# A graph network with routed experts on one core: four PSUM banks for the next table's chunks, one-hots handed over by rising counts, the second layer's weights summed on VectorE

## The reference

```python
xn = _layernorm(x, axis=-1)
# graph part, for l in range(2), on xn:
W = jnp.einsum('rb,bio->rio', coeffs[l], bases[l])      # 8 relations from 30 bases
h = jnp.einsum('ni,rio->rno', x, W)
msg = h[edge_type, src] * deg_inv[dst][:, None]
agg = jax.ops.segment_sum(msg, dst, num_segments=num_nodes)
x_new = agg + x @ self_loops[l]                         # relu after the first layer
# attention part, on xn: q, k = elu(.) + 1; kv = k^T v; out = q kv / (q . k_sum)
x = x + graph(xn) + attention(xn)
# experts, on layernorm(x): idx = argmax(xf @ router_w.T + router_b)
x = x + relu(relu(xf @ W1[idx] + b1[idx]) @ W2[idx] + b2[idx])
```

## Time and profile before

| | |
|---|---|
| median of 3 runs | 3629.47 us (3622.14 to 3641.18) |
| the profiled execution | 3602.8 us, its span 3601.1 us |
| granted TensorE clock, mean | 0.822 |
| busy | PE 68%, PEld 49%, DVE 26%, ACT 18%, POOL 46% |
| startup | 0 to 385 us |
| first layer | 385 to 1985 us |
| second layer | 1985 to 3275 us |
| experts | 3340 to 3601 us |

### The profile page before, as it was taken

One profiled execution on the slowest core, in us unless ns is written; L12 is line 12 of the kernel. 1 busy time (PEld: TensorE's weight loads), 2 busy tenths in 40 slices (PEclk: granted clock), 3 DMA queues, 4 the chain that ended last, 5 costly groups with the idle time before them and its releaser, 6 DMA issues. The chain is left out here.

```text
span 3601.1 us, 37652 instructions
## 1 busy us (share of the span) xinstructions
PE 2442.1 (68%) x9592; PEld 1750.2 (49%) x9592; DVE 924.5 (26%) x2885; ACT 657.0 (18%) x1423; POOL 1648.2 (46%) x1712
## 2 busy tenths in 40 slices
PE   6999356667666667766669166666766666657197
PEld 3777234445444445444446154544545445445065
DVE  2120112222222222222223032332323323224233
ACT  4455111111111111111112001111112111110033
POOL 0000554455444554444540655555655556652534
PEclk9999778888888888888889577777777878778577
DMA  8655533333333333333331323333332333321441
GB/s 221 223 222 190 163 105 110 111 105 115 109 106 105 105 117 107 111 110 106 114 111 73 110 84 89 88 90 87 89 92 85 91 91 89 92 82 45 130 128 53
DMA packets 155518, 401.32 MB, mean 111 GB/s; under 512 B 35102, under 2 KB 86657, under 8 KB 140348
## 3 DMA queue, kind: packets, MB, share of 16 engines
q0 software_dynamic: 81648, 219.65, 21.0%
q10 hardware_dynamic: 36156, 126.22, 9.1%
q1 hardware_dynamic: 37585, 53.92, 5.5%
HBM read 262.69 MB, written 141.04 MB: 112 GB/s over the span
## 5 line engine op out<-in xcount | busy, mean ns | idle before, releaser
L487 POOL DMA_INDIRECT gnn_ring<-table,g_idx x1564 | 1511.8, 967 | 1604.7 <-PE gnn_pagg L530 840.0
L530 PE MATMUL gnn_pagg<-gnn_ring,gnn_oh 128*128 x3904 | 1125.3, 432 | 387.4 <-issue 337.2
L530 PEld LDWEIGHTS gnn_pagg<-gnn_ring,gnn_oh 128*128 128x128 f32 x3904 | 779.5, 213 | 723.0 <-issue 615.3
L514 DVE TENSOR_TENSOR gnn_oh<-gnn_col,g_dst 128x256 f32<-128x256 f32 x976 | 408.0, 425 | 1510.9 <-DVEq L49 1344.8
L711 PE MATMUL gnn_pm<-gnn_whigh,gnn_high 128*128 128x512 f32 x392 | 209.0, 533 | 369.2 <-ACT gnn_rows L762 269.1
L711 PEld LDWEIGHTS gnn_pm<-gnn_whigh,gnn_high 128*128 128x128 f32 x392 | 98.7, 252 | 422.1 <-ACT gnn_rows L762 291.0
L1014 ACT ACTIVATE gnn_qe<-gnn_pq,gnn_bq 128x128 f32<-128x128 f32 x98 | 36.0, 367 | 1062.9 <-remote 1019.0
L711 PE MATMUL gnn_pm<-gnn_wlow,gnn_high 128*128 128x512 f32 x392 | 195.2, 498 | 0.0
L711 PE MATMUL gnn_pm<-gnn_whigh,gnn_low 128*128 128x512 f32 x392 | 194.7, 497 | 0.0
L762 ACT COPY gnn_rows<-gnn_pm 128x512 f32<-128x512 f32 x196 | 110.7, 587 | 449.4 <-DMA pre_bs<-in_L_gnn_bases 257.1
L366 PE MATMUL pre_psum<-pre_whigh,pre_high 128*128 128x512 f32 x392 | 159.4, 407 | 10.6 <-DVE pre_low L294 7.0
(11 more groups left out here) (172 smaller groups left out, 2320.0 us busy)
## 6 DMA issues: line engine op xcount, KB each, us to landing
table<-pre_rows ACTq DMA_DIRECT2D x49, 1024.0 KB, 3.9
table<-gnn_rows ACTq DMA_DIRECT2D x48, 1024.0 KB
gnn_ring<-table,g_idx POOLq DMA_INDIRECT x1564
pre_bs<-in_L_gnn_bases SPq DMA_DIRECT2D x64, 240.0 KB
bucket<-gnn_zrow SPq DMA_DIRECT2D x16, 650.0 KB
g_xT<-bucket SPq DMA_DIRECT2D x20, 520.0 KB, 6.3
x1T<-gnn_x1T ACTq DMA_DIRECT2D x49, 128.0 KB
gnn_x1T<-x1T ACTq DMA_DIRECT2D x49, 128.0 KB
```

Of the source, the lines that this page charges most:

```text
L487: eng.indirect_dma_start(self.ring[:, q % RG, t, 0:D], None, self.g.table[self.l][:, :], bass.IndirectOffsetOnAxis(ap=self.g.idx[:, at:at ...
L514: self.nc.vector.tensor_tensor(self.oh[:, h, :, :], self.col[:, :].unsqueeze(1).to_broadcast([P, n, P]), self.g.dst[:, ds(q * TPG + h * n, ...
L530: mm = nc.tensor.matmul(pagg[:, k, 0:self.width], self.oh[:, h, i, :], self.ring[:, ds(q & (RG - 1), 1), t, 0:self.width].rearrange("p o n ...
```

## The change

1. The products of a block in the first layer get four PSUM banks, one for each chunk (`pm`, `NC = 4`). `chunk_free` and its waits are gone. The transposes `pT` lose their own bank and are written to the fourth bank of `pm`; `turn(b)` waits for `rows_ok` of the block before. `pagg` has one bank in place of two in the first layer.
2. `oh_ok` and `oh_free` are no more decremented: their counts rise through the layer, and the loops wait for `q + b + 1`, worked out from the loop's register. `pairs` is gone; the gate waits for `oh_free` of the second half.
3. The second layer's relation weights (used in `gnn_first`) are made on VectorE: 240 terms, base times coefficient added to a tile `wr` that stays in SBUF, spread over the startup's blocks: 7 beside most blocks, 3 or 1 beside those with layernorm work, 0 beside two. `wrel`'s second half, its 8 pieces on TensorE and ScalarE and its reload are gone. SyncE loads 30 whole bases.
4. In `gnn_first` VectorE makes the weights' low part behind block 0, and TensorE waits for it ahead of block 1.

The core of the diff:

```diff
     def onehots(self, eng, b, seq):
             for h in range(HALF):
-                take(eng, self.oh_free[h])
+                eng.wait_ge(self.oh_free[h], q + b + 1)
...
     (sum)
             for h in range(HALF):
-                take(eng, self.oh_ok[h])
+                eng.wait_ge(self.oh_ok[h], q + b + 1)
                 for i in range(n):
...
-                    if t == 0:
-                        mm.then_inc(self.pairs, 1)
-                    elif i == n - 1:
-                        mm.then_inc(self.oh_free[h], 1)
+                mm.then_inc(self.oh_free[h], 1)
...
     (gathers)
-                eng.wait_ge(self.pairs, last)
+                eng.wait_ge(self.oh_free[HALF - 1], last)
...
     (gnn_first)
-        pm = s.ps("pm", [P, W, 512])
+        pm = s.ps("pm", [P, NC, 512])
-        pT = s.ps("pT", [P, 512])
+        pT = pm[:, NC - 1, 0:D]
...
-            def multiply(k):
+            def multiply(b):
                 reach(eng, low_ok)
-                for n in range(2 * W):
-                    reach(eng, chunk_free)
+                for n in range(NC):
...
-            def turn():
+            def turn(b):
                 reach(eng, xn_ok)
+                if b:
+                    eng.wait_ge(rows_ok, b)
...
-            eng.wait_ge(wr_in, WEIGHTS_IN)
             for h in range(H2):
-                nc.scalar.copy(whigh[:, h, :], rows[:, h, :]).then_inc(split_ok, 1)
+                nc.scalar.copy(whigh[:, h, :], wr[:, h, :]).then_inc(split_ok, 1)
...
     (startup)
+        def terms_beside(b):
+            return 0 if b in (0, 2 * G) else 1 if chunk_at(b) else 3 if chunk_at(b - 1) else 7
...
+            def terms(lo, hi):
+                for i in range(lo, hi):
+                    n, r = divmod(i, R)
+                    if r == 0:
+                        eng.wait_ge(base_in[n % AT_ONCE], 16 * (n // AT_ONCE + 1))
+                        if n:
+                            eng.wait_ge(added, n)
+                        else:
+                            eng.wait_ge(cr_in, 16)
+                    w = wr[:, :, r * D:(r + 1) * D]
+                    if n:
+                        ins = V.scalar_tensor_tensor(out=w, in0=base[:, n % AT_ONCE, :, :], scalar=cr[:, i:i + 1], in1=w,
+                                                     op0=ALU.mult, op1=ALU.add)
+                    else:
+                        ins = V.tensor_scalar(w, base[:, 0, :, :], cr[:, i:i + 1], None, ALU.mult)
+                    if r == R - 1:
+                        ins.then_inc(added, 1)
...
                 multiply(b)
-                if piece_after(b) is not None:
-                    weights(piece_after(b))
                 if b + AHEAD < NB:
                     turn(b + AHEAD)
```

More of the change, by code:

```diff
@@ L96, in __init__ @@
         self.dve_own, self.scattered = s.sem("dve_own"), s.sem("scattered")
-        self.agg_sems = {n: s.sem(n) for n in ("groups_in", "gate", "ring_ok", "agg_ok", "agg_free",
-                                               *(f"oh_ok{h}" for h in range(HALF)), *(f"oh_free{h}" for h in range(HALF)))}
+        self.agg_sems = {n: s.sem(n) for n in ("groups_in", "gate", "ring_ok", "agg_ok", "agg_free")}
         dram = lambda name, shape, dt: nc.dram_tensor(name, shape, dt).ap()
@@ L184, in startup @@
         dve_own = g.dve_own
-        bases = [a["L0_gnn_bases"][l].rearrange("b (q i) o -> q b (i o)", q=4) for l in range(2)]
+        cr_in, added = s.sem("cr_in"), s.sem("added")
+        base_in = [s.sem(f"base_in{k}") for k in range(AT_ONCE)]
+        bases = a["L0_gnn_bases"][0].rearrange("b (q i) o -> q b (i o)", q=4)
         block = ctx.enter_context(nc.Block())
@@ L197, in stage @@
             return xs[0:4 * R, at:at + PIECE // D, :].rearrange("p b d -> p (b d)")
-        def piece_after(b):
-            c, late = divmod(b - EVERY - 1, EVERY)
-            return NPC + c if late == 0 and 0 <= c < NPC else None
+        def terms_beside(b):
+            return 0 if b in (0, 2 * G) else 1 if chunk_at(b) else 3 if chunk_at(b - 1) else 7
+        first_terms = [min(NBASE * R, sum(terms_beside(c) for c in range(b))) for b in range(NB + 1)]
+        assert first_terms[NB] == NBASE * R
+        done_beside = [next(b for b in range(NB) if first_terms[b + 1] >= R * (n + 1)) for n in range(NBASE)]
+        base_at = [max(n, done_beside[n - AT_ONCE] + 1) if n >= AT_ONCE else n for n in range(NBASE)]
         @block.sync
@@ L235, in _ @@
                     rows_in(b // G + 2)
-                if b % EVERY == 2 and b // EVERY < NPC:
-                    load(NPC + b // EVERY)
+                if b == 0:
+                    eng.dma_start(cr[:, :], a["coeff_rows"].rearrange("(o n) -> o n", o=1).to_broadcast([P, NBASE * R])).then_inc(cr_in, 16)
+                for n in range(NBASE):
+                    if base_at[n] == b:
+                        if n >= AT_ONCE:
+                            eng.wait_ge(added, n - AT_ONCE + 1)
+                        eng.dma_start(base[:, n % AT_ONCE, :, :], a["L0_gnn_bases"][1][n].rearrange("(h p) o -> p h o", p=P)
+                                      ).then_inc(base_in[n % AT_ONCE], 16)
         @block.gpsimd
@@ L332, in _ @@
                     edges()
+                terms(first_terms[b], first_terms[b + 1])
+            eng.wait_ge(added, NBASE)
         @block.tensor
@@ L396, in weights @@
             def weights(n):
[L397 to L400 removed]
+                if n >= WB:
+                    eng.wait_ge(w_out[n % WB], 16 * (n // WB))
                 for q in range(4):
@@ L443, in _ @@
                 eng.wait_ge(stored[k], 16 * ((NB + 1 - k) // 2))
-            for k in range(WB):
-                eng.wait_ge(w_out[k], 16 * (NPC // WB + (NPC // 2 if k < 2 else 0)))
 class Aggregate:
@@ L462, in __init__ @@
         self.agg_ok, self.agg_free = sems["agg_ok"], sems["agg_free"]
-        self.oh_ok = [sems[f"oh_ok{h}"] for h in range(HALF)]
-        self.oh_free = [sems[f"oh_free{h}"] for h in range(HALF)]
+        self.oh_ok = [s.sem(f"oh_ok{h}") for h in range(HALF)]
+        self.oh_free = [s.sem(f"oh_free{h}") for h in range(HALF)]
     def groups_of(self, eng, b):
@@ L499, in begin @@
             ins.then_inc(self.ring_ok, 1)
-    def end(self, eng):
-        for h in range(HALF):
-            take(eng, self.oh_free[h])
     def onehots(self, eng, b, seq):
@@ L663, in _ @@
             seq(ins)
-            for h in range(H2):
-                eng.wait_ge(split_ok, h + 1)
-                ins = V.tensor_tensor(wlow[:, h, :], rows[:, h, :], whigh[:, h, :], ALU.subtract)
-            ins.then_inc(split_ok, 1)
             eng.wait_ge(kv_in, 80)
@@ L670, in _ @@
                 step(b, b % 2)
-            agg.end(eng)
+                if b == 0:
+                    for h in range(H2):
+                        eng.wait_ge(split_ok, h + 1)
+                        ins = V.tensor_tensor(wlow[:, h, :], wr[:, h, :], whigh[:, h, :], ALU.subtract)
+                    ins.then_inc(split_ok, 1)
             eng.wait_ge(kv_done, 1)
@@ L1268, in program @@
         had = nc.snapshot_sems()
-        startup(nc, g, a)
-        nc.clear_and_free_semaphores(nc.allocated_since(had))
-        nc.all_engine_barrier()
-        gnn_first(nc, g, a)
+        with nc.sbuf_tensor("second_wr", [P, H2, R * D], F32) as wr:
+            startup(nc, g, a, wr)
+            nc.clear_and_free_semaphores(nc.allocated_since(had))
+            nc.all_engine_barrier()
+            gnn_first(nc, g, a, wr)
         r = Routed(Scope(nc, ctx, "rt"))
```

108 lines of the change are left out of this document (48 added, 60 removed).

## The result

| | before | changed |
|---|---|---|
| median | 3625.8 us (3619.0 to 3641.18, 4 runs) | 3484.89 us (3471.86 to 3495.94, 4 runs) |
| profiled execution, span | 3602.8, 3601.1 us | 3479.84, 3477.8 us |

What follows compares the result with a forecast made beforehand. TensorE bounds the startup; in the first layer nothing does, as TensorE's messages come late in gather bursts. Startup -30, first layer's start 0, four banks -181, gate -25: -236, so 3629.5 becomes 3393 us; range 3240 to 3520.

Steps and rivals of the forecast that it cites:

- Startup, -30: Startup: eight weight pieces leave TensorE's path, VectorE's terms at 0.689 us each stay hidden: -30 us (to +80).
- Start of the first layer, 0 (-10 to +7): First layer's block 0: TensorE starts some 10 us sooner, but the chain ends by the burst's end anyway: 0.
- Four banks: First layer: the product's 24 matmuls run unbroken, period falls from 31.8 to 27.5 us over 42 periods: -181 us.
- a: First layer: lateness of L537's message after the loop, 3.1 us before, taken as 6 on average; 3 best.
- from there to the product: First layer: the way from VectorE's first use (L633) to the product (L711), taken as 4.3 us.
- a clock above 0.92: First layer, profile after: TensorE's clock was to rise above 0.92, from 0.86, as a sign of success.
- Quick and slow blocks mix: First layer: a longer block gets its gate in quiet time and is early again; period between 24.4 and 31.8 us.
- Counts, 0: Both layers' 490 groups: the gap of 0.54 us may grow or shrink by 0.1, +-49 us; taken as 0.
- Gate in the second layer, -25: Second layer: gathers' gate opens 0.8 us sooner at each of 49 gates, between -39 and 0: -25 us.
- rival 1: First layer: the wait moves to L537's message, a is 10, period 31.5 us; 3580 us, chance 0.18.
- Rival 2: First layer: L537's message waits for the burst's full release, period 36.6 us; slower, 3776 us, chance 0.10.
- Rival 3: Startup: VectorE becomes the bound, a term costing over 0.75 us; at 1.0 us +59, 3480 us, chance 0.06.

Runs made afterwards that it cites:

- b: The changed kernel with the four banks undone, counts and VectorE's weights kept, on a chip with prompt messages: 2587.8 us, ratio 0.9917 to the kernel before.
- c: The changed kernel with four banks and counts both undone, only VectorE's weights kept, on a chip with prompt messages: 2582.0 us, ratio 0.9895 to the kernel before.
- g: The changed kernel as it is, run again on a chip with late messages: 3353.3 us, ratio 0.9323 to the kernel before.
- i: The changed kernel with the first layer's transposes put ahead of the projection, on a chip with late messages: 3373.9 us, ratio 0.9396 to the kernel before.
- s: The changed kernel with the four banks undone, counts and VectorE's weights kept, on a chip with late messages: 3471.3 us, ratio 0.9643 to the kernel before.
- t: The changed kernel in which the projection sends no message of its own, on a chip with late messages: 3381.6 us, ratio 0.9395 to the kernel before.
- h: The changed kernel with the one-hot counts undone, four banks and VectorE's weights kept, on a chip with late messages: 3417.1 us, ratio 0.9489 to the kernel before.

## Why the prediction was right or wrong

**Startup, -30: right.** It gave 27.0 us. The term of a weight was put too low, 0.689 where it took 0.748 us, so a plain block has 7 x 0.748 + 0.42 = 5.66 us of VectorE work in a TensorE block of 5.65. The cover is gone to the last tenth; TensorE still was busy 243 of 250 us. An eighth term would have made VectorE the bound.

**Start of the first layer, 0 (-10 to +7): wrong, +9.** TensorE did start sooner, and with it block 0's loop went into the first burst from its 8th microsecond. Four rows of the changed kernel:

```profile
365.62 0.21 PE L542 MATMUL gnn_pagg<-g_zero 128*128 128x2 bf16 x1
399.44 0.42 DVE L533 TENSOR_TENSOR gnn_oh<-gnn_col,g_dst 128x256 f32<-128x256 f32 x1 [10.78 <-DMA g_bound<-bounds]
412.37 0.21 PE L553 MATMUL gnn_pagg<-g_zero 128*128 128x2 bf16 x1
434.36 0.16 DVE L647 TENSOR_SCALAR gnn_dm<-gnn_pagg 128x1 f32<-128x1 f32 x1 [24.00 <-remote]
```

The loop took 46.8 us where it had taken 12.4, and L647 then came 22 us late where it had been 14. VectorE's 4.49 us for the low parts now stood in the chain ahead of block 1 as well. The step said that the chain ends by the burst's end whatever its start. Here ScalarE had the transposes 93.5 us after the first gather, at the end of the burst, and the product and the low parts came behind it; before it had them 67.2 us after. No run separates the early start from the low parts.

**Four banks: the mechanism right, its neighbour missed.** The wait between the chunks went, and I asked what is late next. I named L537's message and nothing else, and put the way from there to the product at a fixed 4.3 us. In the block shown it is 9.1 us, because the transposes' message is late as well, and the product itself takes 8.1 where I had 6.2, much of it at the low clock. The working, in us:

| term | forecast | block shown | mean of 44 periods | the same before |
|---|---|---|---|---|
| loop | 10.9 | 9.6 | 11.5 | 10.6 |
| a, to VectorE's first use | 6 | 3.3 | 4.2 | 2.4 |
| from there to the product | 4.3 | 9.1 | 7.2 | 5.3 |
| product, to the next sum | 6.2 | 8.1 | 7.2 | 13.8 |
| period | 27.4 | 30.1 | 30.0 | 32.0 |

The third line is the failed term. It need not have been missed: the 4.3 was read off one block, and over all periods before it was 5.3, with the transposes' message 2.0 us late. The value of a that I thought uncertain, 6, was 3.3 in most blocks and 4.2 on average. It stayed because L553 didn't move: the gate opened 0.8 us sooner in the block, as expected, and the loop got shorter by as much, which was not, so the sum still ended 6.8 us into the burst and not 7.6. Here is the luck: with a at 4.2 and the other terms as forecast the period would be 25.6 us and the time near 3315 us (an estimate by the forecast's own sum), 170 us from the measured one where 3393 is 92 away. The 6 paid for a part of what was missed. The sign named for the stage, a clock above 0.92, did not show: 0.85, where it was 0.86.

**Quick and slow blocks mix: right, for a reason not given.** I expected a long block to be followed by an early gate. It is the quick block that harms the next, by letting its loop run into the burst that the quick block itself began. The burst begins at 2.8 us, lasts 20.0 and lets go 2.7 us later, which makes 25.5 us, an estimate of the shortest block that doesn't harm the next. In the trace the bound lies higher: behind blocks of 24.8 to 27.9 us the loop took 10.2 to 16.3 us, behind those of 28.4 us and more 9.6 to 10.3 (block 40 with its 24 gathers apart).

**Counts, 0: too low on the late chips.** The loop of a common block of the first layer became 0.9 us shorter (medians of 9.6 against 10.5 us), though blocks whose loop ran into a burst took that back in the mean. The runs put the counts at 64 us on top of the banks; of this the forecast had the gate's 25. The Trainium skill (TensorE: Matmul & The Clock Gate, The cost: per-tile semaphore tail) has 26.3 ns for each increment; for one in each of 490 groups that is an estimate of 13 us. No run here shows it. On the prompt chip b, with counts, took 2587.8 and c, without, 2582.0 us, no gain, but there the gathers set the period (20.1 to 20.2 us with counts and without), and a TensorE quicker by 13 us would not show. On the late chip the 64 us are more than those 13.

**Gate in the second layer, -25: wrong in the first measurement (-3), borne out later.** The periods of that layer were uneven before (17 to 48 us) and stayed so (14 to 38), with a mean of 26.0 where it was 26.1. On the other late chips it is 25.3 to 25.4 in the four traces with counts (g, i, s, t) and 26.1 in h without them, 33 us in 47 periods. ScalarE's first copy of a block still follows the start of its burst by 23.0 us (median), as forecast. Which part of the counts is the gate's was not tried, and why the first measurement shows nothing of it is open.

**The last 9 us**, behind the start of the second layer's block 48 and mostly in the experts' part, which no edit touches, were not forecast and are not explained.

**The rivals.** In rival 1's sum the other end, without the gate's part, is -43 (13 and 30), which makes 3586 us, and not -15. Rival 1 (the wait moves to the release) is half of what happened: the wait moved, but behind L553's message, not to it. Rival 2 happened in single blocks only: block 8 took 41.4 us. Rival 3 stood at its threshold (0.747 us a term, and 0.748 measured) without costing anything yet. Missing among them was that the lateness belongs to the chip. With it gone the same change is worth 1%, and on g's chip it was worth 239 us, what I had forecast for the first.

## What to carry to other kernels

When a wait goes, list every later hand-over of the same kind as the one that made it long, each with its own price, before the chain between them is called fixed; here two messages of one engine were late and only one was priced. Where a burst of other work makes hand-overs late, a block that gets quicker moves its successor into that burst, so read periods in pairs, not alone. And a wait that is microseconds longer than the work behind it may belong to the chip: measure the kernel before on more than one before tuning it away.
